# A fused attention and feed-forward layer whose weighting catches up one unit of lag over seven units of a pass, in halves of 256 queries

## The reference

```
xn  = layernorm(x)
q, k, v = split(xn @ in_proj_weight.T + in_proj_bias)      # 16 heads of 16
scores  = (q / sqrt(16)) @ k.T                             # per head, 2048 x 2048
scores  = -inf where  i - 16 <= j <= i                     # a band of 17 keys is left out
x1  = x + (softmax(scores) @ v) @ out_proj_weight.T + out_proj_bias
out = x1 + tanh(layernorm(x1) @ weight @ aux_weight1 @ aux_weight2 + bias)
```

## Time and profile before

| what | value |
|---|---|
| median of three runs | 2109.38 us |
| the profiled execution, its own time | 2111.1 us |
| its span on the core | 2106.8 us |
| first exponential of the stream | 88.4 us from the span's start |
| ScalarE busy | 1927.0 us (91%) |
| TensorE busy, matmuls | 1838.3 us (87%) |
| VectorE busy | 697.8 us (33%) |
| mean granted TensorE clock | 0.974 |

### The profile page before, as it was taken

How to read it: one execution, slowest core, us unless ns; L and a number is a source line. 1 busy time by engine, 2 the same in 40 slices (tenths; PEclk the granted TensorE clock), 3 DMA queues, 4 the chain that set the end, 5 groups by cost and what they waited for, 6 DMA issues and landing times. The chain is left out here.

```text
span 2106.8 us, 100654 instructions
## 1 busy us (share of the span) xinstructions
PE 1838.3 (87%) x47072; PEld 759.1 (36%) x47072; DVE 697.8 (33%) x1366; ACT 1927.0 (91%) x2106; POOL 151.7 (7%) x172
## 2 busy tenths in 40 slices
PE   6599999999889999999889999999978889798872
PEld 3233343343334434343333434343332323232321
DVE  5223333334233343433324333333322112121212
ACT  3499999999889999999889999999979999999970
POOL 2000000001000010100101010100000000000000
PEclk9799999999999999999999999999989999999996
DMA  3410102110340110201341020201241010101000
GB/s 122 128 30 20 56 26 63 31 52 29 55 87 26 57 36 18 65 23 59 56 87 33 20 64 23 61 26 53 45 62 41 8 47 16 46 16 35 19 28 24
DMA packets 85023, 94.38 MB, mean 45 GB/s; under 512 B 15786, under 2 KB 73578, under 8 KB 84594
## 3 DMA queue, kind: packets, MB, share of 16 engines
q1 hardware_dynamic: 84596, 87.83, 16.5%
HBM read 53.09 MB, written 26.25 MB: 38 GB/s over the span
## 5 line engine op out<-in xcount | busy, mean ns | idle before, releaser
L1149 ACT ACTIVATE probs<-scores 128x1024 f32<-128x1024 f32 x2048 | 1888.8, 1109 | 77.2 <-PE scores L1172 74.9
L1191 PE MATMUL outs<-probs,vs 64*32 64x512 f32 x16384 | 1089.9, 593 | 21.6 <-issue 21.6
L1172 PE MATMUL scores<-qs,ks 49*32 49x512 f16 x16384 | 850.2, 384 | 166.9 <-ACT probs L1149 144.8
L1172 PEld LDWEIGHTS scores<-qs,ks 49*32 49x32 f16 x16384 | 237.0, 89 | 1087.0 <-ACT probs L1149 1040.0
L1191 PEld LDWEIGHTS outs<-probs,vs 64*32 64x32 f32 x16384 | 305.8, 106 | 60.8 <-issue 35.2
L860 DVE TENSOR_TENSOR probs<-probs,allowed 128x320 f32<-128x320 f32 (+2 forms) x280 | 151.7, 545 | 328.0 <-ACT probs L1149 327.8
L1230 PE MATMUL spare<-s_xt,w_qkv 64*32 64x256 f32 x3072 | 120.9, 376 | 0.0
L1230 PE MATMUL spare<-w_o,ctx_in 64*32 64x256 f32 x2048 | 80.2, 383 | 21.0 <-DVE ctx_in L885 19.4
L809 POOL TENSOR_TENSOR s_squares<-s_qk_f 128x512 bf16<-128x512 f32 x48 | 61.4, 1279 | 354.5 <-DVE s_qk_f L927 354.5
L803 POOL TENSOR_TENSOR s_x<-s_x,bias_o 128x1024 f32<-128x1024 f32 x16 | 38.2, 2386 | 655.1 <-DMA s_x<-in_x 655.1
L1230 PE MATMUL spare<-w_ffn,s_f_xt 64*32 64x256 f32 x2048 | 81.3, 384 | 3.0 <-DVE s_pre L1032 1.6
(11 more groups left out here) (103 smaller groups left out, 771.0 us busy)
## 6 DMA issues: line engine op xcount, KB each, us to landing
qs<-q_parts SPq DMA_DIRECT2D x192, 64.0 KB
ks<-k_parts SPq DMA_DIRECT2D x36, 256.0 KB
ctx_in<-raw SPq DMA_DIRECT2D x256, 32.0 KB
inverse<-row_inverse SPq DMA_DIRECT2D x32, 256.0 KB
s_x<-in_x SPq DMA_DIRECT2D x16, 512.0 KB, 6.9
out<-s_pre SPq DMA_DIRECT2D x16, 512.0 KB, 6.0
s_xin<-in_x SPq DMA_DIRECT2D x12, 512.0 KB, 7.7
q_parts<-s_parts SPq DMA_DIRECT2D x24, 256.0 KB, 2.2
```

What stands on the lines that cost most here:

```text
L1149: act.activation(probs[:, u % RING, 2 * slot:2 * slot + 2].rearrange("p c q -> p (c q)"), scores[:, 2 * slot:2 * slot + 2].rearrange("p c ...
L1172: last = pe.matmul(scores[cols, 2 * slot + e], ks[rows, group, keys], qs[rows, group], start=True, stop=True)
L1191: last = pe.matmul(outs[32 * c:32 * c + 32, side], vs[keys, at:at + 2 * HD], probs[keys, u % RING, c], start=(i == 0), stop=(i == KBLOCKS ...
```

## The change

`weighed_at` now gives triples: a unit and a range of its 512 queries. In the first pass of a step the lag is made up between `i` 11 and 17, in the second between 10 and 16 (`CATCH_UP`). At the first of these positions the unit four back is weighed whole between the scores, and the first 256 queries of the unit three back behind them. At the five that follow, the last 256 queries of the unit four back are weighed between the scores and the first 256 of the unit three back behind them. At the last, the last 256 queries of the unit four back stand between the scores and the whole unit three back behind them. All else goes as before. The semaphore `summed` goes up when the last queries of a unit have been weighed.

```
+CATCH_UP = ((11, 17), (10, 16))

         def weighed_at(position):
-            i = position % KBLOCKS
+            hg, i = divmod(position % STEP, KBLOCKS)
+            first, last = CATCH_UP[hg]
             base = position - i
             if i < 3:
-                found = [base - 3 + i]
+                found = [(base - 3 + i, 0, CHUNK)]
             elif i == 3:
                 found = []
-            elif i < 13:
-                found = [position - 4]
-            elif i == 13:
-                found = [position - 4, position - 3]
+            elif i < first:
+                found = [(position - 4, 0, CHUNK)]
+            elif i == first:
+                found = [(position - 4, 0, CHUNK), (position - 3, 0, EMB)]
+            elif i < last:
+                found = [(position - 4, EMB, CHUNK), (position - 3, 0, EMB)]
+            elif i == last:
+                found = [(position - 4, EMB, CHUNK), (position - 3, 0, CHUNK)]
             else:
-                found = [position - 3]
+                found = [(position - 3, 0, CHUNK)]

-            def weigh(u):
+            def weigh(u, lo, hi):
-                        last = pe.matmul(outs[32 * c:32 * c + 32, side], vs[keys, at:at + 2 * HD],
-                                         probs[keys, u % RING, c], start=(i == 0), stop=(i == KBLOCKS - 1))
-                last.then_inc(summed, 1)
+                        last = pe.matmul(outs[32 * c:32 * c + 32, side, lo:hi], vs[keys, at:at + 2 * HD],
+                                         probs[keys, u % RING, c, lo:hi], start=(i == 0), stop=(i == KBLOCKS - 1))
+                if hi == CHUNK:
+                    last.then_inc(summed, 1)
```

More of the change, by code:

```diff
@@ L670, in weighed_at @@
         def weighed_at(position):
-            i = position % KBLOCKS
+            hg, i = divmod(position % STEP, KBLOCKS)
+            first, last = CATCH_UP[hg]
             base = position - i
             if i < 3:
-                found = [base - 3 + i]
+                found = [(base - 3 + i, 0, CHUNK)]
             elif i == 3:
                 found = []
-            elif i < 13:
-                found = [position - 4]
-            elif i == 13:
-                found = [position - 4, position - 3]
-            else:
-                found = [position - 3]
-            return [u for u in found if 0 <= u < NCH * STEP]
+            elif i < first:
[6 more added lines that the diff above has]
+                found = [(position - 4, EMB, CHUNK), (position - 3, 0, CHUNK)]
+            else:
+                found = [(position - 3, 0, CHUNK)]
+            return [w for w in found if 0 <= w[0] < NCH * STEP]
         def finishing(step, r):
@@ L1174, in score @@
                 last.then_inc(scored, 1)
-            def weigh(u):
+            def weigh(u, lo, hi):
                 b, qc, hg, i, kb = unit(u)
-                if i == 0:
+                if i == 0 and lo == 0:
                     if u:
@@ L1340, in run_step @@
                     if due:
-                        weigh(due[0])
+                        weigh(*due[0])
                     score(u, 1)
                     for w in due[1:]:
-                        weigh(w)
+                        weigh(*w)
                     if projects:
```

## The result

The changed kernel takes 2134.27 us (median of 6 runs, 2128.17 to 2139.70) against 2107.33 (6 runs, 2105.52 to 2113.48) for the kernel before. The ratio is 1.0122 with a 95% interval of 1.0099 to 1.0145: 27 us slower, where the forecast was 11.6 and its range ended at 2132. The profiled execution took 2137.18 us, 26 more than that of before, at a mean granted clock of 0.972 (0.974 before).

A forecast was written before the change was run, and what follows sets the result against it. ScalarE's exponentials, 0.917 us each, were taken to bound the kernel. The terms -6.7 (double units), +1.1 and +1.9 (lateness) and +15.3 (instructions) sum to +11.6, so 2109.4 becomes 2121.0 us, range 2106 to 2132.

The forecast's parts named there:

- The mechanism and its sign: On TensorE, added instructions use up blocks of 256 before the next arrives, so ScalarE waits: slower, chance 0.54.
- part 5: 6144 added TensorE instructions, 24 blocks: 23.5 us of pauses at r 12 to 17 and 42 to 48, costing +15.3 us.
- The large starvations: Six TensorE stalls at key loads: put at nothing; rival that they move, up to 3 us each in three, chance 0.12.
- What bounds the kernel: ScalarE's exponentials, 0.917 us each, set the pace; TensorE's order matters only where ScalarE falls behind.
- Parts 1 to 4: The new order on TensorE: double units go, halves cost nothing, late scores cost 1.1 and 1.9 us; together -3.7 us.
- Part 4: Steps 12 to 15, r 48 with a feed-forward piece: scores late by 0.3 and 0.16 us, +1.9 us in all.
- The half's duration: Weighing 256 queries on TensorE takes 0.43 us, half of 0.86; bounds 0.43 and 0.86.
- The share that ScalarE sees: ScalarE loses 0.65 of TensorE's pause time: 23.5 us of pauses give +15.3 us.
- double units: Units of the kernel before with two weighings, each losing 0.21 us; removing them in 32 passes gives -6.7 us.
- lateness: Late scores at the last of the seven positions: +1.1 us over 28 passes, +1.9 us in steps 12 to 15.
- Fetch stays hidden: Rival: instruction packets arrive in time on TensorE, so only -3.7 us remains: 2105.7 us; chance 0.30.
- All pauses are seen: Rival: TensorE has no slack, ScalarE loses every pause, upper bound 26 us: 2131.7 us; chance 0.08.

The follow-up runs named there:

- h1: Changed kernel with half of the matmuls of each 256-query half left out, so about as many instructions as the kernel before; 2105.55 us against 2109.60, ratio 0.9984.
- p2: Changed kernel with the key transfers at each change of sequence spread out instead of issued at once; 2090.71 us.
- p1: Kernel before with the twelve key transfers at each change of sequence spread out instead of issued at once; 2066.21 us against 2109.60, ratio 0.9793.
- e1: Kernel before, order kept, with weighings at the twelve positions issued as two halves in place; 2130.18 us against 2105.97, ratio 1.0101.
- e2: Kernel before with as many weighings halved as in e1, at twelve positions without projection pieces in steps 0 to 11; 2119.08 us, ratio 1.0058.

## Why the prediction was wrong

The mechanism and its sign were right. The step that failed is the size of part 5, the price of the added instructions: +15.3 us in the sum, some 21.7 in the trace. The large starvations, put at nothing, may have added to the miss.

*What bounds the kernel.* Right. ScalarE's exponentials stayed at 1890 us, and what grew is the time in which it waits for scores.

*Parts 1 to 4, -3.7 us.* Right as far as can be told. h1 measures -3.4, though not clear of its interval and with less work for TensorE. In the first passes of the kernel after that have no pause the seven positions lose 0.05 to 0.06 us in all. Part 4 is seen in step 13, r 49:

```profile
1798.67 1.07 ACT L1155 ACTIVATE probs<-scores 128x1024 f32<-128x1024 f32 x1
1799.95 1.02 ACT L1155 ACTIVATE probs<-scores 128x1024 f32<-128x1024 f32 x1 [0.21 <-PE scores L1178]
1801.02 1.02 ACT L1155 ACTIVATE probs<-scores 128x1024 f32<-128x1024 f32 x1
```

The first two ends, 1799.74 and 1800.97, are 1.23 apart, the next, 1802.04, is 1.07 behind: 0.31 and 0.15 over 0.917, where 0.3 and 0.16 were forecast.

*The half's duration.* Right: TensorE, step 5, r 43 and 44, from the start of a half to the next group 795.06 - 794.63 = 0.43.

```profile
794.63 0.62 PE L1197 MATMUL outs<-probs,vs 64*32 64x256 f32 x16
795.06 0.69 PE L1281 MATMUL spare<-w_qkv,s_xt 64*32 64x128 f32 x32
```

*Part 5, the pauses.* This is the step that failed, by size. I had 23.5 us more of small pauses. The trace has 40.1 - 6.8 = 33.3. At r 12 to 18 it is 18.6 - 2.9 = 15.7 for 13.6 forecast, at r 42 to 50 15.5 - 1.3 = 14.2 for 10, and 3.4 in places where I had none, mainly r 7 to 9 and r 53 to 60. The last are units whose instructions did not change, with blocks of two units at 128 that last 3.67 us, inside the 3.2 to 4.7 of the quiet pauses; their edges moved, and more of them now fall badly. The estimate of 0.6 us a step at r 42 to 48 was too low for two reasons. A quiet block was taken to come in 3.3 to 3.7 us, and those that TensorE waited for came in up to 4.7. And there are two dense pairs of units there, and a block often spans either; I had counted one pause.

*The share that ScalarE sees.* 0.65 held by this count. The loss away from key loads rose by (86.7 - 53.1) - (63.6 - 50.5) = 20.5 us. Of that 1.9 followed on a large starvation in step 12, 6.1 of double units went and 3.0 of lateness came, so pauses account for 20.5 - 1.9 + 6.1 - 3.0 = 21.7 of 33.3, again 0.65. The 21.7 stand on the ends of exponentials; the share does not stand as firmly, since with the strict count of pauses it would be 0.7 to 0.8.

*The large starvations.* I put them at nothing, on the ground that the last edge in steps 3, 7 and 11 is again where it was. The large pauses rose from 39.1 to 46.9 us and the loss near key loads by 2.7 (0.6 of double units came off there), with the 1.9 in step 12: 5.2 us. In step 7 the pause came at r 48 instead of 51, one edge before the one that the argument was about:

```profile
1052.74 1.03 ACT L1155 ACTIVATE probs<-scores 128x1024 f32<-128x1024 f32 x1 [8.98 <-PE scores L1178]
```

against 8.21 before. One pair of traces doesn't settle this term: p2 stands to p1 as the change to the kernel before without any such starvation, and e1, with the same instructions, loses 49.5 us near the key loads, no more than the kernel before. So whether this term is scatter or phase stays open.

Together, for the profiled executions: -3.7 + 21.7 + 5.2 + 0.3 (29 doubles counted instead of 32, with the rest near key loads) is 23.5 in the stream (measured from its first to its last exponential: 23.0), and the stream's later start and the tail account for the other 2.7 of 26. The forecast of 11.6 thus missed 6.4 by the pauses, 5.2 by the starvations and 2.7 outside the stream.

*The rivals.* "Fetch stays hidden" fell: the pauses came, and e1 puts 24 us on the instructions. The Trainium skill, "Runtime: NRT & Kernel Launch", section "Instruction fetch mechanics", calls the cost of crossing a 16 KiB boundary of the instructions mostly hidden. This case's traces don't agree where blocks are short: TensorE stood at the edge of a block that came 3.45 us after the edge before with idle DMA engines, and 6.1 us under the burst. "All pauses are seen" gave 2131.7, close to the 2134.27 measured, by a wrong way: the pauses grew beyond the sum, and not all of them were seen. Its 40 us of pauses don't follow from the text either. 0.4 us on each of the 24 added blocks makes 33, and 40 needs 41 blocks, which the prediction doesn't name. The chance for slower, 0.54, was too timid: I took the best value where the spread of arrivals pointed upwards.

What stays open is why the changed kernel is 2.7 us above e1 and not 3.7 below it, as e1 plus the forecast gain of the order would have it. The difference of some 6 us is within the intervals.

## What to carry to other kernels

In an unrolled kernel count the instructions of the busiest engine per microsecond, in blocks of 256, and set the time in which a block is used up against the time between the edge and the next block's arrival, read from any pause with cause "issue". Here that was 3.2 to 4.7 us in quiet and mostly 4.5 to 6.9 under the burst, so cutting float32 matmuls in two in units of up to 160 instructions cost 24 us (e1), where the smoother order was worth some 4. And before the order of an engine is refined, look for the large pauses: spreading the twelve key transfers of each change of sequence, which were queued six at a time, won 43 us with no change of the work.

## What was not expected of the hardware

Losses don't only come where instructions are added. With 24 blocks more in the whole kernel, pauses appeared at r 7 to 9 and 53 to 60, where nothing had changed, and e2, which in steps 0 to 11 adds 32 instructions only to units of 64, cost 13 us. A stretch whose blocks last 3.67 us has no reserve against arrivals of 3.2 to 4.7.

The wait of a packet goes with the data that are queued at that moment: the same 1.5 MB in 18.79 us instead of 3.66 us of issues took every large pause of the weight loads away. None that is left there is over 2 us, except one of 2.52 at r 55 of step 7, where ScalarE idled 3.29. The rate in GB/s is a poor guide to it: the starved packets of before waited while the queue moved 113 to 124 GB/s, the burst at r 13 and 14 of step 5 moved 344 and held its packet up by far less.
